# Two score banks for the last turned tiles, and the other work spread over two more places

## The reference

```
xn  = layernorm(x)
out = x + ssm(xn) + attention(xn) + experts(xn)

ssm:       u = xn @ W_in + b_in; causal 4-tap convolution; linear scan with
           a 16 x 16 state (tanh(A)); silu; @ W_out + b_out
attention: q, k, v = xn @ W_qkv + b_qkv; 16 heads of 16 channels
           softmax(q k^T / 4) v
experts:   gate = softmax(xn @ W_gate + b_gate); the best 2 of 8 experts
           sum of gate * (xn @ W_experts + b_experts) over these two
```

## Time and profile before

| what | us |
|---|---|
| median of three runs | 824.97 |
| the profiled execution | 831.9 |
| its span | 830.1 |
| TensorE busy | 783.4 (94%) |
| VectorE busy | 583.2 (70%) |
| ScalarE busy | 530.0 (64%) |
| GpSimd busy | 391.2 (47%) |

### The profile page before, as it was taken

One profiled execution on the slowest core, in us unless ns is written; L12 is line 12 of the kernel. 1 busy time (PEld: TensorE's weight loads), 2 busy tenths in 40 slices (PEclk: granted clock), 3 DMA queues, 4 the chain that ended last, 5 costly groups with the idle time before them and its releaser, 6 DMA issues.

```text
span 830.1 us, 13136 instructions
## 1 busy us (share of the span) xinstructions
PE 783.4 (94%) x4368; PEld 450.1 (54%) x4368; DVE 583.2 (70%) x834; ACT 530.0 (64%) x916; POOL 391.2 (47%) x531
## 2 busy tenths in 40 slices
PE   8799989998999999999999999999999999999995
PEld 6356555555555655555555655565555554554542
DVE  4567866976679756886568866797668967578720
ACT  3436756775666756667467756767667765766764
POOL 6534644563345723456235634456235453343542
PEclk9769999999999999999999999999999999999997
DMA  8401101122010311102211031113111111112100
GB/s 273 88 2 41 39 5 37 40 67 63 20 42 18 86 44 40 37 5 74 56 40 41 12 86 34 39 39 90 40 40 40 37 55 26 44 31 64 34 2 26
DMA packets 32497, 39.30 MB, mean 47 GB/s; under 512 B 8639, under 2 KB 18661, under 8 KB 32430
## 3 DMA queue, kind: packets, MB, share of 16 engines
q1 hardware_dynamic: 31102, 36.71, 16.9%
q0 software_dynamic: 512, 0.95, 0.7%
q10 hardware_dynamic: 816, 0.80, 0.4%
HBM read 8.18 MB, written 4.19 MB: 15 GB/s over the span
## 4 chain that ended last, share of the span: by engine, by line
PE 78%; DVE 14%; issue 3%; DMA 2%; ACT 1%; SPq 1%; POOL 0%; ACTq 0%; POOLq 0%; DVEq 0%
PE PS L421 41%; PE SB L547 13%; PE PS L577 10%; DVE mx L974 10%; PE TB L561 6%; PE PS L471 4%; PE PS L437 2%; DVE ys L830 1%; DVE xl L862 1%; DMA Pt<-in_wvg 1%; DMA kst<-qkl 1%; PE PS L519 1%; PE PS L505 1%; DVE qkl L856 1%; PE PS L433 1%
## 5 line engine op out<-in xcount | busy, mean ns | idle before, releaser
L974 DVE TENSOR_REDUCE mx<-SB 128x2 f32<-128x1024 f32 x256 | 313.0, 1223 | 186.2 <-PE SB L547 185.7
L1028 POOL TENSOR_TENSOR acc<-acc,mt 128x256 f32<-128x256 f32 x320 | 249.0, 784 | 240.7 <-ACT mt L625 155.2
L764 ACT ACTIVATE Pt<-TB 128x1024 f32<-128x1024 f32 x256 | 262.5, 1025 | 40.6 <-PE TB L561 37.5
L625 ACT ACTIVATE mt<-PS,cpad 128x256 f32<-128x256 f32 x256 | 107.5, 470 | 92.7 <-PE PS L421 90.8
L547 PE MATMUL SB<-kst,qst 48*128 48x512 f32 x512 | 130.5, 506 | 22.2 <-DVE mx L974 16.5
L577 PE MATMUL PS<-Pt,V 128*17 128x512 f32 x1024 | 138.7, 614 | 1.1 <-ACT Pt L764 1.1
L547 PEld LDWEIGHTS SB<-kst,qst 48*128 48x128 f32 x512 | 48.4, 186 | 128.5 <-DVE mx L974 64.3
L421 PE MATMUL PS<-weh,xTh 128*128 128x512 f32 x256 | 110.9, 433 | 4.8 <-DVE qkl L856 1.7
L561 PE MATMUL TB<-qst,kst 50*128 50x512 f32 x512 | 105.5, 407 | 3.9 <-ACT Pt L764 3.0
L421 PE MATMUL PS<-wel,xTh 128*128 128x512 f32 x256 | 101.3, 396 | 0.0
L421 PE MATMUL PS<-weh,xTl 128*128 128x512 f32 x256 | 100.8, 394 | 0.0
(11 more groups left out here) (145 smaller groups left out, 1151.7 us busy)
## 6 DMA issues: line engine op xcount, KB each, us to landing
qst<-qkh SPq DMA_DIRECT2D x124, 64.0 KB, 2.2
kst<-qkh SPq DMA_DIRECT2D x124, 64.0 KB, 2.2
out<-acc SPq DMA_DIRECT2D x8, 512.0 KB, 2.9
qst<-qkl SPq DMA_DIRECT2D x62, 64.0 KB, 2.2
kst<-qkl SPq DMA_DIRECT2D x62, 64.0 KB, 2.2
acc<-in_x SPq DMA_DIRECT2D x7, 512.0 KB, 3.8
Bt<-in_wexp SPq DMA_DIRECT2D x2, 512.0 KB, 7.0
raw<-in_wexp SPq DMA_DIRECT2D x2, 512.0 KB, 8.9
```

The lines of the kernel that those rows point to most:

```text
L625: return e.activation(mt[:, item % NM, :], P, ACT.Copy, scale=scale)
L764: e.activation(Pt[:, T % NP, :, :], TB[:, :, :], ACT.Exp, scale=0.25).then_inc(s_ex, 1)
L974: e.tensor_reduce(mx[:, g % 2, 0:2, 4 * jj + a], SB[:, :, :], AX.X, ALU.max).then_inc(s_mx, 1)
L1028: e.tensor_tensor(v, v, mt[:, item % NM, :], ALU.add).then_inc(s_mt, 1)
```

## The change

Of the eleven turned tiles that are computed after the last score tile's step (245 to 255) the last ten go in turn to the banks of `SB`, which have no score tile any more, and to those of `TB`: the even ones to `SB`. Tile 246 waits for the maxima of the last score tile; each tile after it waits for the exponential of the tile two places before it rather than of the one before. The exponential reads the bank of its tile. And the planner's `last` goes from 264 to 266.

```
+FREE = STEPS - LAG + 1
...
-    last, spent = STEPS + LAG - 3, 0.0
+    last, spent = STEPS + LAG - 1, 0.0
...
+        def turned_bank(t):
+
+            return SB if t >= FREE and (t - FREE) % 2 == 0 else TB
...
             def turned(t):
                 g, a, jj = t // 8, t % 8 // 2, t % 2
-                if t:
-                    e.wait_ge(s_ex, t)
+                if t == FREE:
+                    e.wait_ge(s_mx, STEPS)
+                elif t:
+                    e.wait_ge(s_ex, t - (t > FREE))
                 else:
                     e.wait_ge(s_kp, 1)
...
-                    ins = e.matmul(TB[:, h, :], kst[rows, g % 3, jj, 128 * a:128 * a + 128], qst[rows, g % 3, jj, :],
+                    ins = e.matmul(turned_bank(t)[:, h, :], kst[rows, g % 3, jj, 128 * a:128 * a + 128], qst[rows, g % 3, jj, :],
...
-                    e.activation(Pt[:, T % NP, :, :], TB[:, :, :], ACT.Exp, scale=0.25).then_inc(s_ex, 1)
+                    e.activation(Pt[:, T % NP, :, :], turned_bank(T)[:, :, :], ACT.Exp, scale=0.25).then_inc(s_ex, 1)
```

## The result

The changed kernel takes 0.9947 of the time of before (95% interval 0.9927 to 0.9967): 4.4 us less, with 2.7 to 6.0 us as the bounds. The medians of 20 runs each are 823.41 and 827.67 us. The forecast was 2.5 us less, 822.5 in a range of 820.2 to 826.8. The direction was right, the size small, just outside that interval.

What follows compares the result with a forecast made beforehand. TensorE, busy 94% of the span, was taken as the bound, so only its idle time or clock could move the end. Tail -2.1, body +0.5 and clock -0.86 gave -2.5 us: 824.97 to 822.5, range 820.2 to 826.8.

Steps and rivals of the forecast that it cites:

- The banks: Turned tiles after step 256: alternating banks alone take off 1.6 us, though values still wait for exponentials (0.7 and 0.4 us).
- The tail's idle time: Step 256 to last turned tile: banks plus moved units take 2.1 of 2.5 us idle, bounds 1.2 and 2.5.
- The body: Steps 0 to 255: losing one or two units adds 0.5 us idle, bounds 0 and 1.6 for each emptied even step.
- The late part: Steps 226 to 255: units beyond one per even step stand in odd steps and leave first; values steps lose them for nothing.
- The clock: At the end: last values at the high clock, 0.86 us saved, transposes left as they are; bounds 0 and 1.3 us.
- The sum: Whole kernel: tail -2.1, body +0.5, clock -0.86 make -2.5 us, giving 822.5 us.
- Half of it: Rival: in the tail, values' wait replaces the turned tile's and the clock falls as before; 823.8 us, chance 0.12.
- Slower: Rival: emptied even steps in the body also bring the clock down, 3.3 us each; 827.5 us, chance 0.15.
- The fourth: Rival: turned tiles in bursts of two, then idle, bring a low-clock stretch before step 266; 825.0 us, chance 0.05.

Runs made afterwards that it cites:

- e1_banks: The full change with the planner's `last` taken back to 264, so only the alternating banks stay, every unit where it stood before; ratio 0.9940 against the kernel before.
- e3_late_spread: The full change, but the planner aims at 264 up to step 225 and at 266 from there; ratio 0.9962 against the kernel before.
- e4_empty_evens: The full change with three single expert units moved from even steps 90, 94 and 98 to 91, 95 and 99; ratio 0.9988 against the kernel before.
- l267_filled: The full change with `last` at 267 and one output unit each moved from steps 115 and 147 into empty steps 114 and 146; ratio 0.9891.
- e5b_fill4: The kernel before plus 4 unused identity matmuls after each of turned tiles 253 and 255; last values' start to the end 7.35, not 8.67 us.
- e2_spread: The kernel before with only `last` at 266, all turned tiles still in TB; tail idle falls by 0.66 us, the end is 0.84 us shorter.
- after_again: The full change unaltered, run again beside its two parts on the same chip; ratio 0.9956 against the kernel before.
- e7_best: The full change with two units one step earlier (257, 258) and the last values started before the last exponential; step 256 to transposes 26.05 against 26.15 us.

## Why the prediction was right, and where it was off

*The banks.* Right in mechanism and size (`e1_banks`): 1.6 us by hand, 1.55 measured with the units in place, and the two waits that the values inherit.

*The tail's idle time.* 2.1 us off 2.5 was the forecast; idle up to the last turned tile's end fell to about 0.6 us, 1.9 less. What was left over was not the forecast 0.4 us of values waiting in step 261 (an M stands in step 260 now), but the transfer of the maxima rows, which the prediction had not looked at. Eight or nine M behind the last score tile were forecast; eight units came, seven M and an O, the last in step 264 (the planner's `left` at step 256 is 21.9, not 22.7).

*The body.* This is the step that failed: "+0.5 us" of idle was forecast, and 1.1 (second profile) to 1.9 us (first) went away. The late part went as argued: steps 226 to 255 are idle for 3.62 us, 0.35 more. But the shift of the pace changes the order from step 19 on. That filled four even steps (26, 114, 142 and 174), each idle for 1.6 us before (with the odd step behind it), took away the idle time of steps 24 and 104 (1.7 and 1.9 us), and emptied 110, 146 and 178, now idle for 1.5 to 1.6 us each; step 48 has 0.7 us more. The prediction named this as open either way and gave it no value. `e1_banks` and `e3_late_spread`, which have the old order, keep the old idle time, and `e4_empty_evens` and `l267_filled` give the price of an empty even step, 1.07 and 1.45 us, within its bounds.

*The clock.* 0.86 us were forecast with the transposes left at the low level. They kept the high one too in the full change: 1.29 us, near the upper bound of 1.3. `e5b_fill4` shows 1.32 with no other gain. In `e2_spread`, `e3_late_spread` and `e4_empty_evens` it is 0.85: there the clock fell between the values and the transposes. Which of the two an execution gets is not decided by the kernel alone: `after_again` and `e4_empty_evens` have the same tail, and an end of 7.36 and 7.81 us. So 0.86 in the forecast was as good a value as 1.29: which of the two the first profile had was luck.

*The sum.* With the sizes of the profiles it is -1.9 in the tail, -1.1 to -1.9 in the body and -1.3 at the end: -4.3 to -5.1 us, and the timed runs say -4.4. About 0.8 us of the body's time is not placed: in `after_again` steps 19 to 255 hold a unit of 1.5 us less than before, with the same 17 us at the low clock, but are busy for only 0.7 us less.

*The rivals.* "Half of it" is what `e1_banks` would have looked like without the clock. "Slower" needed two new empty steps with a stretch at the low clock behind each. There were three new ones, and the low clock did follow 178 in both profiles, and 110 in the first (3.4 us from 382.8). What kept this rival from coming true is that the new order also filled four even steps, so that four are empty and not five, and that falls of before's profile in steps 53, 104 and 115 went. The price of 3.3 us for such a step lies within what was seen: 1.07 us without a fall, 3.3 with 110's, 5.0 with 178's. The fourth, taken from the Trainium skill's "TensorE: Matmul & The Clock Gate" ("A second HAM failure mode"), did not come: with the tiles in turn in two pairs of banks the granted clock from step 256 to the last values is 1.00.

Whether the clock in mid-kernel gained from the change is open. The timed runs' mean clock rose from 0.973 to 0.979; a good part of that is the end (in before's trace the last 9.6 us of the span are at 0.50, in after's the last 2.9), and between step 19 and step 256 the profiles of before and `after_again` both have 17 us at the low level, that of after 20. Over all fourteen profiles it is 6.8 to 20.5 us, of which about half is lost. `e1_banks` shows the price, as it has the order of before in these steps and the same idle time, but 10.2 us at the low level and not 17.1: it takes 3.3 us less for them (before, then `e1_banks`):

```profile
96.58:796.29 699.71, 673.57 (x3851) 383.97 (x3851) 517.61 (x709) 465.22 (x788) 328.01 (x430) 0.99 0.17 43
95.49:791.86 696.37, 670.15 (x3852) 382.32 (x3851) 517.23 (x709) 465.79 (x788) 328.69 (x430) 0.99 0.17 43
```

## What to carry to other kernels

When the work that kept a second buffer busy runs out, give its place to the loop that is left, and move other work into that loop's waits: by the profiles' idle time each of the two brought less alone. A planner's constant that spreads work also reorders everything before; look at the steps that it empties or fills one by one, because in this kernel each was worth 1.1 to 1.6 us, as much as the banks alone gave. And compare stretches between the same steps, not spans: here 4.0 of the 7.5 us between two profiles lay ahead of the first changed step.

## What the runs showed that I had not expected

Two of the four matmuls of a values step take as long as all four. (The program issues four, `for j in range(4)`, and they show as eight rows; the section on the kernel before calls them eight.) They write to four different blocks of 17 partitions of one bank, from partition 0, 32, 64 and 96. In `e7_best` the weight loads of the last two begin at 814.54, and the copy that waits for them starts at 815.63, 1.09 us later; in the full change all four started at 815.23, and the copy at 816.35, 1.12 us later.

```profile
814.54 0.12 PEld L590 LDWEIGHTS PS<-Pt,V 128*17 128x17 f32 x4 [1.01 <-ACT Pt L777]
815.63 0.59 ACT L786 COPY ot<-PS 128x512 f32<-128x512 f32 x1 [1.14 <-PE PS L590]
```

They run side by side, so splitting them buys nothing.

A float32 matmul of 128x128 by the identity takes 0.22 to 0.24 us at the high clock (16 of them 3.84 us, 4 of them 1.16 us) and shows as two rows.
